# A two-layer mixture-of-experts kernel: the expert tiles' first weights in four buffers, and the gate and residual of the second layer on GpSimd

## The reference, cut to what matters

```
layer 0:  y_k = gelu(h @ w_fc[e_k] + b_fc[e_k]) @ w_proj[e_k] + b_proj[e_k]     (k = 0, 1)
          x   = x + gate * (g_0 * y_0 + g_1 * y_1)
layer 1:  y   = relu(h @ W1[e] + b1[e]) @ W2[e] + b2[e]
          x   = x + gate * g * y
```

## Time and profile before

| | |
|---|---|
| median of 3 runs | 504.24 us (501.85 to 504.29) |
| the profiled execution's own time | 505.9 us |
| its span | 504.2 us |
| busy: PE / DVE / ACT / POOL | 338.1 / 311.7 / 176.4 / 158.4 us |
| expert tiles of layer 0 | from about 199 to 334 us of the span |
| expert tiles of layer 1 | from about 435 to 493 us |

### The profile page before, as it was taken

One profiled execution on the slowest core, in us unless ns is written; L12 is line 12 of the kernel. 1 busy time (PEld: TensorE's weight loads), 2 busy tenths in 40 slices (PEclk: granted clock), 3 DMA queues, 4 the chain that ended last, 5 costly groups with the idle time before them and its releaser, 6 DMA issues.

```text
span 504.2 us, 7928 instructions
## 1 busy us (share of the span) xinstructions
PE 338.1 (67%) x2189; PEld 247.4 (49%) x2190; DVE 311.7 (62%) x912; ACT 176.4 (35%) x340; POOL 158.4 (31%) x240
## 2 busy tenths in 40 slices
PE   2856899789648897769999964540670700498880
PEld 1742238332323325669999953440360700388770
DVE  6888947894498933845656521346697780175770
ACT  1034532247111670334545420264504420153430
POOL 9222841900343441130000176422000047134360
PEclk9985555557955597789999985575785555599995
DMA  2699100000000001022222222115600002333320
GB/s 70 162 392 361 60 1 0 1 0 6 23 26 26 22 27 42 15 75 62 57 68 63 72 72 59 47 38 161 235 0 1 1 31 102 87 71 76 74 54 0
DMA packets 36217, 34.57 MB, mean 69 GB/s; under 512 B 6259, under 2 KB 26949, under 8 KB 36192
## 3 DMA queue, kind: packets, MB, share of 16 engines
q1 hardware_dynamic: 32432, 26.83, 17.5%
q0 software_dynamic: 3712, 7.44, 5.0%
q10 hardware_dynamic: 48, 0.00, 0.0%
HBM read 19.92 MB, written 14.79 MB: 69 GB/s over the span
## 4 chain that ended last, share of the span: by engine, by line
PE 43%; DVE 25%; issue 7%; ACT 6%; another core or an unknown queue 6%; POOL 3%; DVEq 2%; DMA 1%; SPq 0%; ACTq 0%; POOLq 0%
PE ps L1100 10%; PE ps L1111 10%; PE ps L938 6%; DVE mx L1589 4%; PE ps L933 4%; PE ps L913 3%; POOL rows L507 3%; PE ps L960 2%; ACT wide L659 2%; DVE stats L1236 2%; PE ps L889 2%; PE ps L1090 1%; DVE w_now L1720 1%; DVE wide L1812 1%
## 5 line engine op out<-in xcount | busy, mean ns | idle before, releaser
L507 POOL DMA_INDIRECT rows<-token_rows,posu x48 | 52.1, 1085 | 154.3 <-DVE token_rows L1512 65.1
L1100 PE MATMUL ps<-xsT,w_now 128*128 128x128 f32 x552 | 83.0, 299 | 20.9 <-issue 11.5
L1728 DVE TENSOR_TENSOR hb<-ps,b_in 128x512 f32<-128x512 f32 x69 | 47.6, 689 | 79.4 <-PE ps L1100 55.0
L1100 PEld LDWEIGHTS ps<-xsT,w_now 128*128 128x128 f32 x552 | 73.9, 209 | 27.1 <-issue 14.9
L1111 PE MATMUL ps<-w_out,hg 128*128 x552 | 79.6, 292 | 9.1 <-issue 4.9
L1111 PEld LDWEIGHTS ps<-w_out,hg 128*128 128x128 f32 x552 | 72.6, 206 | 11.1 <-issue 11.1
L742 ACT ACTIVATE hg<-hb 128x512 f32<-128x512 f32 x69 | 43.3, 629 | 47.5 <-DVE hb L1728 40.4
L1589 DVE TENSOR_REDUCE mx<-ps 128x2 f32<-128x512 f32 (+2 forms) x48 | 44.4, 948 | 4.7 <-PE ps L913 4.3
L520 POOL DMA_INDIRECT y<-back,posu x16 | 15.7, 979 | 88.5 <-DMA back<-ys 81.0
L913 PE MATMUL ps<-feat,qs 64*128 64x281 bf16 (+2 forms) x128 | 33.3, 432 | 13.6 <-DVE mx L1589 9.9
L1090 PE MATMUL ps<-ident,xs 128*128 128x128 f32 x69 | 20.1, 300 | 31.5 <-DMA xs<-rows 31.4
(11 more groups left out here) (346 smaller groups left out, 531.4 us busy)
## 6 DMA issues: line engine op xcount, KB each, us to landing
rows<-zeros SPq DMA_DIRECT2D x22, 256.0 KB, 6.9
xs<-rows SPq DMA_DIRECT2D x69, 64.0 KB
back<-ys SPq DMA_DIRECT2D x46, 64.0 KB
w_in<-in_L_ffn_w_fc SPq DMA_DIRECT2D x1, 2048.0 KB, 15.1
w_in<-in_L_ffn_W SPq DMA_DIRECT2D x1, 2048.0 KB, 8.4
rest<-rows SPq DMA_DIRECT2D x23, 65.0 KB
token_rows<-in_L_attn_x SPq DMA_DIRECT2D x1, 832.0 KB, 8.8
wmod<-in_L_wmod SPq DMA_DIRECT2D x2, 384.0 KB, 4.4
```

Of the source, the lines that this page charges most:

```text
L507: pool.indirect_dma_start(ROWS[l], bass.IndirectOffsetOnAxis(ap=posu[:, k, j:j + 1], axis=0), token_rows[:, j, 0:WIDTH[l]], None).then_inc ...
L1100: mm = pe.matmul(ps[:, c % RING, n * P:(n + 1) * P], w_now[:, c % 2, n * P:(n + 1) * P], xsT[:, c % 2, :], start=True, stop=True)
L1728: v.tensor_tensor(hb[:, c % 2, :].rearrange("p (b t) -> p b t", b=NB), ps[:, c % RING, :].rearrange("p (b t) -> p b t", b=NB), b_in[:, l, ...
```

## The change

Three things are changed, and some semaphores are merged.

1. The copied first weights have four buffers. Two are those of `w_now`, the other two lie in `qs`, which the attention no longer needs. lay_out(t+2) moves ahead of bias_up(t) in DVE's order, and gets a wait of its own, for up(t-2).
2. In layer 1 DVE stops after the bias (`ys_biased`). POOL makes `target`, multiplies `ys` by the gate and adds the residual, as three instructions with a wait for its own result behind each, and then issues the output DMA.
3. PE's down(t) waits for `ys_biased`, SP's load of `rest` for POOL's `ys_ready` and `targets`, SP's store in layer 0 for `ys_biased`.
4. `turned_*`, `hT_*` and `hT_used_*` become one semaphore each for both groups, with offsets (`QUADS`); `vpx_ones` is merged into `stack_clear`, so that the key stack waits for the third of POOL's clears too.

```diff
+        qs_f = qs[:].rearrange("p a n -> p (a n)").bitcast(F32)
+        w_ring = [w_now[:, 0, :], w_now[:, 1, :], qs_f[:, 0:HID], qs_f[:, HID:2 * HID]]
...
# SP, finish(k, c)
-                    sp.wait_ge(sem("ys_ready"), RING * k + (c + 1) + tiles_before(l))
                     if l == 0:
+                        sp.wait_ge(sem("ys_biased"), RING * k + (c + 1))
                         store_tile(k, c)
                     else:
+                        sp.wait_ge(sem("ys_ready"), RING * k + (c + 1))
+                        sp.wait_ge(sem("targets"), RING * k + (c + 1))
                         load_rest(k + 1, c)
...
# POOL, the output of layer 1
             for t in range(T1):
                 r = t % RING
-                pool.wait_ge(sem("ys_ready"), t + 1 + tiles_before(1))
+                pool.wait_ge(sem(f"rest_loaded{r}"), 16 * (t // RING + 1))
+                if t >= RING:
+                    pool.wait_ge(sem(f"ys_sent{r}"), 16 * (t // RING))
+                pool.tensor_scalar(target[:, r:r + 1], rest[:, r, D + 1:D + 2], float(N), None, ALU.add).then_inc(sem("targets"), 1)
+                pool.wait_ge(sem("targets"), t + 1)
+                pool.wait_ge(sem("ys_biased"), t + 1 + tiles_before(1))
+                pool.tensor_scalar(ys[:, r, :], ys[:, r, :], rest[:, r, D:D + 1], None, ALU.mult).then_inc(sem("ys_gated"), 1)
+                pool.wait_ge(sem("ys_gated"), t + 1)
+                pool.tensor_tensor(ys[:, r, :], ys[:, r, :], rest[:, r, 0:D], ALU.add).then_inc(sem("ys_ready"), 1)
+                pool.wait_ge(sem("ys_ready"), t + 1)
                 pool.indirect_dma_start(out_rows, bass.IndirectOffsetOnAxis(ap=target[:, r:r + 1], axis=0),
                                         ys[:, r, :], None, bounds_check=N - 1, oob_is_err=False
                                         ).then_inc(sem(f"ys_sent{r}"), 16)
...
# PE, up and down
-                        mm = pe.matmul(ps[:, c % RING, n * P:(n + 1) * P], w_now[:, c % 2, n * P:(n + 1) * P], xsT[:, c % 2, :],
+                        mm = pe.matmul(ps[:, c % RING, n * P:(n + 1) * P], w_ring[c % RING][:, n * P:(n + 1) * P], xsT[:, c % 2, :],
...
-                        pe.wait_ge(sem("ys_ready"), t - 1 + tiles_before(l))
+                        pe.wait_ge(sem("ys_biased"), t - 1 + tiles_before(l))
...
# DVE, experts(l)
-                def lay_out(c, e):
+                def lay_out(k, c, e):
+                    t = RING * k + c
-                    v.tensor_copy(w_now[:, c % 2, :], w_in[:, bass.ds(e, 1), :].rearrange("p e h -> p (e h)")).then_inc(sem("w_ready"), 1)
+                    if not isinstance(t, int) or t >= RING:
+                        v.wait_ge(sem("h_ready"), t - (RING - 1) + tiles_before(l))
+                    v.tensor_copy(w_ring[c % RING], w_in[:, bass.ds(e, 1), :].rearrange("p e h -> p (e h)")).then_inc(sem("w_ready"), 1)
...
                     ins = v.tensor_tensor(y, ps[:, 6 + c % 2, 0:D], b_out[:, bass.ds(e, 1), :], ALU.add)
-                    if l == 0:
-                        ins.then_inc(sem("ys_ready"), 1)
-                        return
-
                     ins.then_inc(sem("ys_biased"), 1)
-                    v.wait_ge(sem(f"rest_loaded{c % RING}"), 16 * (k + (c // RING + 1)))
-                    r = rest[:, c % RING, :]
-                    v.tensor_scalar(target[:, c % RING:c % RING + 1], r[:, D + 1:D + 2], float(N), None, ALU.add)
-                    v.wait_ge(sem("ys_biased"), t + 1)
-                    v.scalar_tensor_tensor(out=y, in0=y, scalar=r[:, D:D + 1], in1=r[:, 0:D], op0=ALU.mult, op1=ALU.add
-                                           ).then_inc(sem("ys_ready"), 1)
...
                 with v.Fori(1, rounds) as k:
                     e = ids(RING * k - 2, RING + 4)
                     for c in range(RING):
+                        lay_out(k, c + 2, e[c + 4])
                         bias_up(k, c, e[c + 2])
-                        lay_out(c + 2, e[c + 4])
 
                         bias_down(k, c - 2, e[c])
```

More of the change, by code:

```diff
@@ L281, in build_adaln @@
         NTH = {"far": 1, "near": 2, "all": 3}
+        QUADS = {"far": 0, "near": -(-(NT - NA) // 4)}
         ROWS = {0: rows0, 1: rows1}
@@ L413, in _ @@
             sorted_tiles(0)
-            sp.wait_ge(sem("ys_ready"), T0)
+            sp.wait_ge(sem("ys_biased"), T0)
             for k in range(2):
@@ L457, in _ @@
             pool.memset(stack[:, :, 1:2], -1.0).then_inc(sem("stack_clear"), 1)
-            pool.memset(vpx[:], 1.0).then_inc(sem("vpx_ones"), 1)
+            pool.memset(vpx[:], 1.0).then_inc(sem("stack_clear"), 1)
             pool.memset(zeros[:], 0.0).then_inc(sem("zeros_set"), 1)
@@ L682, in router_rows @@
                     n = min(4, hi - lo - 4 * q) * P
-                    act.wait_ge(sem("turned_" + g), q + 1)
+                    act.wait_ge(sem("turned"), QUADS[g] + q + 1)
                     if q >= 2:
-                        act.wait_ge(sem("hT_used_" + g), q - 1)
+                        act.wait_ge(sem("hT_used"), QUADS[g] + q - 1)
                     act.activation(hTr[:, q % 2, 0:n], ps[:, TURN_BANK[g] + q % 2, 0:n], ACT.Identity, scale=modcol[0][:, CB:CB + 1],
-                                   bias=modcol[0][:, SB:SB + 1]).then_inc(sem("hT_" + g), 1)
+                                   bias=modcol[0][:, SB:SB + 1]).then_inc(sem("hT"), 1)
             def gap_exp(g):
@@ L697, in _ @@
                     router_rows("far")
-                    act.wait_ge(sem("hT_used_far"), 4)
+                    act.wait_ge(sem("hT_used"), 4)
                     act.copy(lg[:, NA:NT, :], ps[:, LOGIT_BANK["far"], 0:(NT - NA) * NE].rearrange("p (j e) -> p j e", e=NE)
@@ L1029, in turn @@
                     if q >= 2:
-                        pe.wait_ge(sem("hT_" + g), q - 1)
+                        pe.wait_ge(sem("hT"), QUADS[g] + q - 1)
                     for j in range(4 * q, min(4 * q + 4, hi - lo)):
                         mm = pe.transpose(ps[:, TURN_BANK[g] + q % 2, (j % 4) * P:(j % 4 + 1) * P], xn[:, lo + j, :], ident[:])
-                    mm.then_inc(sem("turned_" + g), 1)
+                    mm.then_inc(sem("turned"), 1)
                 turn(0)
@@ L1039, in router0 @@
                         turn(q + 1)
-                    pe.wait_ge(sem("hT_" + g), q + 1)
+                    pe.wait_ge(sem("hT"), QUADS[g] + q + 1)
                     for j in range(4 * q, min(4 * q + 4, hi - lo)):
@@ L1043, in router0 @@
                                        cols[:, ROW_ROUTER:NROW], start=True, stop=True)
-                    mm.then_inc(sem("hT_used_" + g), 1)
+                    mm.then_inc(sem("hT_used"), 1)
             def count(g):
@@ L1199, in _ @@
                     router1(g)
-            router1(NT // 4 - 1).then_inc(sem("hT_used_all"), 1)
+            router1(NT // 4 - 1).then_inc(sem("logits1"), 1)
             count("all")
@@ L1407, in _ @@
             head_norm(gl_c, NA, 1.0 / HD, LN_EPS, weight=4)
-            v.wait_ge(sem("stack_clear"), 2)
+            v.wait_ge(sem("stack_clear"), 3)
             signal(split(NA, K_FIRST, K_COPIES), "k_stack", 1)
@@ L1430, in read_logits @@
                 if experts == 2:
-                    v.wait_ge(sem("hT_used_" + g), -(-n // 4))
+                    v.wait_ge(sem("hT_used"), QUADS[g] + -(-n // 4))
                     signal(v.tensor_copy(lg[:, lo:hi, :], pl), "lg_read", NTH[g])
                 else:
-                    v.wait_ge(sem("hT_used_" + g), 1)
+                    v.wait_ge(sem("logits1"), 1)
                     then(v.tensor_tensor(lg[:, lo:hi, :], pl, br_row[:].unsqueeze(1).to_broadcast([P, n, NE]), ALU.add))
@@ L1606, in attend @@
                     v.wait_ge(sem("vp"), 1)
-                    v.wait_ge(sem("vpx_ones"), 1)
+                    v.wait_ge(sem("stack_clear"), 3)
                     then(from_bank(5, 2, vpx[:, :, :, 0:HD].rearrange("p j h o -> p (j h) o")))
@@ L1754, in experts @@
                 e = ids(0, RING + 2)
-                lay_out(0, e[0])
-                lay_out(1, e[1])
+                lay_out(0, 0, e[0])
+                lay_out(0, 1, e[1])
                 if l == 0:
@@ L1766, in experts @@
                         tile_experts("near")
+                    lay_out(0, c + 2, e[c + 2])
                     bias_up(0, c, e[c])
-                    lay_out(c + 2, e[c + 2])
                     if c >= 2:
@@ L1779, in experts @@
                 for t in range(first, T + 2):
+                    if t + 2 < T:
+                        lay_out(0, t + 2, e[t - first + 4])
                     if t < T:
                         bias_up(0, t, e[t - first + 2])
-                    if t + 2 < T:
-                        lay_out(t + 2, e[t - first + 4])
                     bias_down(0, t - 2, e[t - first])
```

## The result

| | before | after |
|---|---|---|
| median of the runs | 504.26 us (501.85 to 508.37, 4 runs) | 531.55 us (530.34 to 535.05, 4 runs) |
| profiled execution / its span | 505.9 / 504.2 us | 535.05 / 533.3 us |
| layer 0's last `ys` starts | 334.02 | 335.76 |
| first and last output DMA start | 445.06, 492.60 | 446.54, 521.71 |
| output's pace per tile | 2.16 us | 75.17 / 22 = 3.42 us |

The kernel became slower: ratio 1.0602, 95% interval 1.0548 to 1.0656. I had said 532. The chip gives some executions of a program a slower state; a ratio here uses the faster ones alone and a median all of them, so the two can differ by some tenths of a percent.

What follows compares the result with a forecast made beforehand. It took POOL's output queue in layer 1, at 3.5 us per tile, to become the bound: -2.2 us in layer 0 and +30.3 in layer 1 make +28.1, so 532 us. The range was 519 to 541 us.

Steps and rivals of the forecast that it cites:

- gap: Layer 1, POOL: time from an output DMA's end to the next tile's destination, taken as 0.15 us between 0 and 0.30.
- release to DMA: Layer 1, POOL: 0.80 us from the add's release to the output DMA's start, forecast as fully exposed in every tile.
- POOL hides part: Rival, layer 1: the DMA's preparation overlaps POOL's own add; pace 2.92 us per tile, time 519.5 us; chance 0.13.
- The lock or a slow PE: Rival, layer 1: SBUF lock by DVE's copies, or PE at a low clock; pace 3.9 us, time 541 us; chance 0.13.
- twice VectorE's time: Layer 1, POOL: page's estimate for the three operations, 0.97 us instead of 1.36; pace 3.1 us, time near 524 us.
- Layer 0's gain: Layer 0: 2.2 us, between 0 and 3.6, from the copy's four buffers and its place before bias_up.
- I take 0.25 us per round: Layer 0's round heads: gain from the earlier copy, between 0 and 0.45 us, counted for seven rounds.
- the 0.18 of before: Layer 0: share of a round's 0.63 us without products that lies at PE's own round head.
- the 0.45 saved at the copy: Layer 0's round heads: PE's 0.21 us idle plus 0.24 us slower product, hanging on the copy; the gain's upper bound.
- first DMA at 445.9 - 2.2: Layer 1's first output DMA: 445.9 us with POOL's operations ahead of it, less layer 0's gain of 2.2 us.
- 1.8 - 0.4: Layer 0: the 1.8 us is the gain forecast for the seven rounds until 289 us, at 0.25 us each.
- carried over 1.7: Whole kernel: the profiled execution was forecast to lie 1.7 us above the median after the change, as before.

Runs made afterwards that it cites:

- e2: Kernel before with only POOL's part of the change (destination, multiply, add in layer 1), two buffers and the old copy order: 531.23 us, ratio 1.0647 to the kernel before.
- e1: Kernel after with layer 1's destination, gate and residual back on DVE, keeping four buffers and the copy ahead of bias_up: 501.48 us, ratio 1.0026 to the kernel before.
- e3: Kernel after without POOL's multiply by the gate and its wait, so the output lacks the gate: 512.21 us, ratio 1.0268 to the kernel before.
- e5: Kernel after with POOL's three operations for tile t+1 issued before the output DMA of tile t: 523.05 us, ratio 1.0435 to the kernel before.
- e9: e1 with PE's loop over 8 tiles instead of 4, DVE's staying at 4: 505.77 us, ratio 1.0117 to the kernel before.
- e4: Kernel after with only the destination on POOL, right before its DMA, gate and residual on DVE: 504.88 us, ratio 1.0131 to the kernel before.
- e6: e4 with the destination of tile t+1 made before the DMA of tile t: 501.20 us, ratio 1.0039 to the kernel before.
- e8: Kernel before with POOL's gathers held back until all 46 tiles of layer 0 are stored: 505.17 us, ratio 1.0039 to the kernel before.
- e7: e1 with DVE's loop over 8 tiles instead of 4, loading 12 registers at a time: 504.16 us, ratio 1.0033 to the kernel before.

## Why the prediction was right, and where it wasn't

**The loss: right in mechanism and size.** POOL becomes the bound, and its pace is the sum of its queue. Term by term, forecast and measured: DMA 1.00 and 1.05, gap 0.15 and 0.08, destination 0.31 and 0.24, its wait 0.09 and 0.10, multiply 0.60 and 0.62, wait 0.09 and 0.08, add 0.45 and 0.45, release to DMA 0.80 and 0.80. 3.49 against 3.42. e2 and e1 show that nothing else of the change is in it, e3 that the terms add, e5 that the 0.80 is whole only because the release comes last.

**The rival "POOL hides part"** (2.92) fell because of the order: e5, which makes the overlap possible, comes to 2.94.

**The lock or a slow PE** (3.9) fell too. PE's clock of 0.85 is a mean: in steps of 5 us it was 1.00 in nine of eleven up to 500 us, 0.77 in the lowest, and 0.50 from 505 us on, when PE had nearly nothing left to do. PE was busy 46.1 of 76.7 us. DVE's copies do cost POOL something where they meet. In the kernel after a copy lies wholly inside a multiply twice:

```profile
468.49 0.80 POOL L610 TENSOR_SCALAR ys<-ys,rest 128x128 f32<-128x128 f32 x1
468.73 0.43 DVE L1739 COPY qs<-w_in 128x512 f32 x1 [2.37 <-PE ps L1116]
```

These two multiplies took 0.80 and 0.81 us, the median is 0.62, and in e2 the longest was 0.89. So a meeting costs 0.2 to 0.3 us, and it was seldom here. The Trainium skill ("SBUF — State Buffer", section "SBUF: two separate sides") says that of a fp32 copy on VectorE and an instruction on GpSimd whichever starts first holds the other off for its whole length. The trace agrees that they disturb each other, but not in the size: the copy started 0.24 us into the multiply and took its usual 0.43. The Trainium skill's page "GPSIMD Engine Reference" (§3.1 and §4.1) with twice VectorE's time was low at this size: (0.62 + 0.45) / 0.35 = 3.1.

**Layer 0's gain: wrong.** The step that failed is "I take 0.25 us per round". The copy did leave PE's path, as the full pace at 239.98 shows. What was late next was mainly not `hg`; it was PE's own round head with its register load, which I had priced at the 0.18 of before and then took as fixed. From the starts of PE's instructions: from the second product before its head to the transpose behind it PE takes 237.08 - 234.48 = 2.60 us at one head and 244.91 - 242.88 = 2.03 at the next, where the full pace is 2 x 0.89 = 1.78 and the kernel before took 237.42 - 235.47 = 1.95. So its own heads cost 0.82 and 0.25 us in turn, some 0.53 on average, and about 0.35 of the 0.45 saved at the copy went there. What was left is 0.06 us a round. e1, with no measurable gain, agrees; e2, with the old order, is back at 8.19; and e9 names the load by making it longer. The load itself is no longer than before (1.00 us in both). Why it is covered less than before, and why only every second head is late, stays open.

**The sum.** Forecast: first DMA at 445.9 - 2.2 = 443.7, last 77.0 later. Measured: 446.54, 75.17 later. So +2.8 and -1.8, and the span came out 1.0 over its forecast of 532.3. Two misses of opposite sign flattered it, and that is luck. Layer 0's last `ys` was due at 334.02 - 2.2 = 331.8 and came at 335.76, 3.9 late. The missing gain up to 287 us is 1.8 - 0.4 = 1.4 of it. The rest lies in the stretch beside the gathers, which differs between executions by more than that. From there to the first DMA it took 1.1 us less than forecast. What lies behind the last DMA stayed: 11.6 us in both. The execution with the trace was itself the slowest of the four, 3.5 us above their median of 531.55, where I had carried over 1.7.

## What to carry to other kernels

Price an engine's queue, not its load: an engine that issues indirect DMAs and waits between them can be busy 68% and still be the bound. If small work must go there, make it for the next tile, so that no DMA waits for the instruction right before it; here that is the difference between e4's 2.09 us and e6's 1.59, and a ratio of 1.0131 against 1.0039. When a wait at a loop's head is removed, look at the same head on the other engines before counting the gain.

## What the runs showed of the hardware that I had not expected

- The 0.80 us from the last release to the start of an indirect DMA, known from the earlier trace rows, is constant: 0.80 or 0.81 in every tile of the kernel after, 0.79 to 0.81 in every tile of e3 and in 18 of 23 of e4. With the release given before POOL's running work, POOL's idle time before the DMA is 0.27 to 0.45 (e5, e6).
- Beside a row of 26 gathers on POOL, 1.39 us apart on average, idle times of 1.9 to 9.2 us that end with a remote release appear on ACT and DVE, and PE's clock is 0.67 over that stretch. Without them the same tiles take 20.5 us instead of 46.8 (e8).
- A register load from SBUF costs by the number: on PE 1.00 us for 4 and 2.00 for 8 (e1, e9), on DVE 1.90 for 8 and 2.79 for 12 (before, e7).
- A weight copy on DVE wholly inside a multiply on POOL makes the multiply 0.2 us longer (0.80 and 0.81 against 0.62) and stays at 0.43 itself.
